# Three of ScalarE's steps cut into parts, and all steps of a hybrid state-space layer placed anew

## The reference

```python
x = x + mamba(layernorm(x))      # D_INNER 256, D_STATE 16, D_CONV 4
x = x + ffn(layernorm(x))
x = x + min_gru(layernorm(x))    # 128 -> 512 -> 128
x = x + ffn(layernorm(x))        # the same weights again
# mamba
xi, z = split(layernorm(x) * gamma + beta @ W_in)
u = silu(conv4(xi) + b_conv)                     # causal, over time
dt = softplus(dt_r @ W_dt + b_dt)                # dt_r, B, C from u @ W_x
h[t] = exp(dt[t] * A) * h[t-1] + dt[t] * u[t] * B[t]
y = (sum over the 16 states of h * C + u * Dskip) * silu(z)
return x + y @ W_out                             # x: mamba's own input
# min_gru
x_in, x_skip = silu(x @ W1 + b1), silu(x @ W2 + b2)
z = sigmoid(x_in @ Wz + bz); h~ = x_in @ Wh + bh
h[t] = (1 - z[t]) * h[t-1] + z[t] * h~[t]        # over time
return (x_skip + h) @ Wo + bo
# ffn: ternary linear 128 -> 512, gelu, ternary linear 512 -> 128,
# each on its input over its root mean square
```

## Time and profile before

| | before |
|---|---|
| median of 3 runs | 849.8 us (848.09 to 851.16) |
| profiled execution | 848.36 us, span 846.6 us |
| instructions | 12621 |
| PE, DVE busy | 705.0 us (83%), 684.5 us (81%) |
| ACT, POOL busy | 641.2 us (76%), 580.7 us (69%) |
| granted PE clock, mean | 0.915 of 2.4 GHz |
| start of the first and of the last scan | 33.92 us, 733.27 us |

### The profile page before, as it was taken

One profiled execution on the slowest core, in us unless ns is written; L12 is line 12 of the kernel. 1 busy time (PEld: TensorE's weight loads), 2 busy tenths in 40 slices (PEclk: granted clock), 3 DMA queues, 4 the chain that ended last, 5 costly groups with the idle time before them and its releaser, 6 DMA issues. The chain is left out here.

```text
span 846.6 us, 12621 instructions
## 1 busy us (share of the span) xinstructions
PE 705.0 (83%) x4116; PEld 596.5 (70%) x4116; DVE 684.5 (81%) x1069; ACT 641.2 (76%) x968; POOL 580.7 (69%) x369
## 2 busy tenths in 40 slices
PE   5666575799789988799789979899799978997995
PEld 4455465578677876588667868688677957786794
DVE  5699989789977998899988998899779988653232
ACT  5787877796899879986899778988898568526403
POOL 4399868777778687877887877968786667513410
PEclk9666677999899999999999999999899979998998
DMA  5521221121111211021112111121111111000000
GB/s 131 184 61 56 75 53 58 51 61 50 32 51 60 63 50 51 27 85 42 50 40 63 63 39 52 41 72 39 50 43 60 50 48 40 2 1 2 13 1 13
DMA packets 35186, 42.81 MB, mean 51 GB/s; under 512 B 7457, under 2 KB 17074, under 8 KB 35122
## 3 DMA queue, kind: packets, MB, share of 16 engines
q1 hardware_dynamic: 35122, 42.00, 16.4%
HBM read 39.63 MB, written 2.36 MB: 50 GB/s over the span
## 5 line engine op out<-in xcount | busy, mean ns | idle before, releaser
L514 POOL TENSOR_TENSOR inflow<-dtu,b_all 128x1024 f32<-128x1024 f32 x127 | 307.7, 2429 | 66.1 <-DVE state L1119 46.6
L1119 DVE TENSOR_TENSOR_SCAN state<-dA,inflow 128x512 f32<-128x512 f32 x256 | 298.3, 1207 | 24.9 <-ACT dA L866 24.5
L866 ACT ACTIVATE dA<-dt,decay_c 128x512 f32<-128x512 f32 x256 | 170.1, 686 | 62.1 <-DVE state L1119 61.2
L1136 DVE TENSOR_TENSOR state<-state,c_ps 128x1024 f32<-128x1024 f32 x128 | 155.6, 1215 | 18.0 <-PE c_ps L1432 13.5
L1441 PE MATMUL y_ps<-ident,state 128*128 128x128 f32 x1024 | 152.2, 298 | 0.0
L1441 PEld LDWEIGHTS y_ps<-ident,state 128*128 128x128 f32 x1024 | 136.1, 155 | 13.9 <-issue 3.8
L1432 PE MATMUL c_ps<-xd,pick 128*128 128x512 f32 x128 | 64.6, 505 | 75.9 <-DVE state L1136 75.8
L1323 PE MATMUL work<-in_hi,wzh_hi 128*128 128x512 f32 x256 | 105.0, 410 | 0.2 <-POOL in_lo L676 0.2
L1324 PE MATMUL work<-in_hi,wzh_lo 128*128 128x512 f32 x256 | 101.3, 396 | 0.0
L1325 PE MATMUL work<-in_lo,wzh_hi 128*128 128x512 f32 x256 | 101.2, 395 | 0.0
L1432 PEld LDWEIGHTS c_ps<-xd,pick 128*128 128x128 f32 x128 | 26.0, 203 | 95.9 <-DVE state L1136 91.3
(11 more groups left out here) (172 smaller groups left out, 1508.3 us busy)
## 6 DMA issues: line engine op xcount, KB each, us to landing
b_all<-b_scratch SPq DMA_DIRECT2D x128, 256.0 KB, 3.2
x_tok<-in_x SPq DMA_DIRECT2D x8, 256.0 KB, 3.7
out_x<-x_tok SPq DMA_DIRECT2D x8, 256.0 KB, 3.6
wide<-in_Wz SPq DMA_DIRECT2D x1, 1024.0 KB, 7.4
...
```

The lines of the kernel that those rows point to most:

```text
L514: eng.tensor_tensor(inflow[:, n % 2, :, tok(b)], dtu[:, :, tok(b)], b_all[:, n % RING, tok(b)].unsqueeze(1).broadcast_to([P, HALVES, TO[b] ...
L866: act.activation(dA[:, h, tok(b)], dt[:, b % 2, h, tok(b)], ACT.Exp, scale=decay_c[:, h, n:n + 1]).then_inc(s_dA[h], 1)
L1119: dve.tensor_tensor_scan(state[:, g % 3, h, tok(b)], dA[:, h, tok(b)], inflow[:, n % 2, h, tok(b)], first, ALU.mult, ALU.add).then_inc(s_s ...
L1136: dve.tensor_tensor(state[:, g % 3, :, tok(b)], state[:, g % 3, :, tok(b)], c_ps[:, tok(b)].unsqueeze(1).broadcast_to([P, HALVES, TO[b] - ...
```

## The change

The two halves of `mix_h_tok` and of `norm_apply` (two tiles each), the two parts of `mix_taps` (u with the first tap, then two taps) and the three parts of `mix_softplus` become operations of their own with places of their own: `h_tok+`, `apply1+`, `taps0+`, `softplus+e`, `softplus+l` and so on. Row 0's softplus stays as it was. What each instruction computes stays, and so do the counts on each engine, but for ACT's table loads: 99 in place of 97. Then all tables have new numbers, `BANK` among them.

```diff
-            def mix_h_tok(b, r, s):
-                act.wait_ge(s_mnb, b + 1)
-                n_tok_free(r, s)
-                for j in tiles(b):
+            def half_tiles(b, part):
+                half = len(tiles(b)) // 2
+                return tiles(b)[part * half:(part + 1) * half]
+
+            def mix_h_tok(b, part, r, s):
+                if part == 0:
+                    act.wait_ge(s_mnb, b + 1)
+                    n_tok_free(r, s)
+                for j in half_tiles(b, part):
...
+            def mix_softplus_exp(b):
+                it = dt[:, b % 2, :, tok(b)]
                 act.wait_ge(s_sparg, HALVES * b + HALVES)
                 act.activation(it, it, ACT.Exp, scale=-1.0).then_inc(s_spexp, 1)
+
+            def mix_softplus_ln(b):
+                it = dt[:, b % 2, :, tok(b)]
                 act.wait_ge(s_spexp, b + 1)
                 act.activation(it, it, ACT.Ln, bias=1.0).then_inc(s_spln, 1)
...
-    "ud": -1, "w12": 1.25, "wzh0": 2.5,
...
+    "ud": -1, "w12": -28.75, "wzh0": 2.75,
...
-    "a.up0": 1, "a.up1": 2, "a.up2": 1, "a.up3": 2, "out": 0, "a.down": 0, "zin0": 2, "zin1": 0, "norm3": 2,
-    "a.sumsq": 1, "d.up0": 1, "d.up1": 2, "d.up2": 2, "d.up3": 1, "norm2": 1, "d.down": 0, "in0": 1, "in1": 2,
...
+    "a.up0": 1, "a.up1": 2, "a.up2": 2, "a.up3": 0, "out": 0, "a.down": 0, "zin0": 2, "zin1": 0, "norm3": 1,
+    "a.sumsq": 2, "d.up0": 2, "d.up1": 1, "d.up2": 2, "d.up3": 1, "norm2": 1, "d.down": 0, "in0": 1, "in1": 2,
```

More of the change, by code:

```diff
@@ L128 @@
-    ("ACT", "d.square3", 1): 42, ("ACT", "h_tok", 1): -21.25, ("ACT", "hi1", 1): 19, ("ACT", "h", 1): -16,
-    ("ACT", "in7", 1): 27.75, ("ACT", "ln_set", 1): -5.75, ("ACT", "silu_u", 1): -8, ("ACT", "silu_z", 1): -2.5,
-    ("ACT", "softplus", 1): -4, ("ACT", "taps0", 1): -12.75, ("ACT", "taps1", 1): -11.5,
-    ("ACT", "z_copy0", 1): -6.75, ("DVE", "apply", 1): -19.75, ("DVE", "d.out", 1): 43.25,
-    ("DVE", "gate", 1): 16.5, ("DVE", "new2", 1): 35.5, ("DVE", "norm", 1): -27.5, ("DVE", "xd_lo", 1): -5,
[9 rows of a table removed]
@@ new lines @@
+    ("DVE", "hid2", 0): 36.25, ("DVE", "hid3", 0): 36.25, ("DVE", "new2", 0): 34.75, ("DVE", "norm", 0): -28.75,
+    ("DVE", "read", 0): 0.25, ("DVE", "scan", 0): -0.5, ("DVE", "stats1", 0): 17.25, ("DVE", "x1", 0): 17,
+    ("DVE", "x2", 0): 25, ("DVE", "x3", 0): 37.5, ("DVE", "xd_lo", 0): -6.25, ("PE", "a.down+", 0): 24.75,
[8 rows of a table added]
+    ("POOL", "base", 0): -17, ("POOL", "conv1", 0): -12.25, ("POOL", "conv2", 0): -13.25,
+    ("POOL", "conv3", 0): -11.5, ("POOL", "d.sum2", 0): 41.75, ("POOL", "h_lo", 0): -7.75,
@@ new lines @@
+    ("DVE", "new1", 7): 34, ("DVE", "new2", 7): 35.25, ("DVE", "new3", 7): 37.25, ("DVE", "norm", 7): -24.75,
+    ("DVE", "read", 7): 0.5, ("DVE", "stats1", 7): 16.75, ("DVE", "stats2", 7): 29, ("DVE", "stats3", 7): 40.5,
[15 rows of a table added]
+    ("POOL", "a.sum2", 7): 24.75, ("POOL", "a.sum3", 7): 24.75, ("POOL", "base", 7): -4.25,
+    ("POOL", "conv3", 7): -12, ("POOL", "d.rms", 7): 48, ("POOL", "d.sum1", 7): 47, ("POOL", "d.sum2", 7): 47,
+    ("POOL", "d.sum3", 7): 47.5, ("POOL", "h_lo", 7): -15.5, ("POOL", "in_lo0", 7): 30,
[3 rows of a table added]
@@ L232 @@
+    ("POOL", "root", 7): -21.5, ("POOL", "x2b", 7): 27.5,
 }
@@ L983, in _ @@
                     mix_softplus(b)
+                for b in due(r, s, ACT_ON["softplus+e"]):
+                    if b > 0:
+                        mix_softplus_exp(b)
+                for b in due(r, s, ACT_ON["softplus+l"]):
+                    if b > 0:
+                        mix_softplus_ln(b)
                 for b in due(r, s, ACT_ON["ud"]):
```

146 lines of the change are left out of this document (76 added, 70 removed), and 234 rows, old and new, of tables (ACT_AT, BANK, DVE_AT, MOVED).

## The result

| | before | changed |
|---|---|---|
| median | 849.8 us (846.6 to 851.2, 20 runs) | 852.0 us (850.0 to 859.0, 20 runs) |
| ratio | | 1.0036 (95%: 1.0023 to 1.0049) |
| profiled execution | 848.36 us | 854.62 us, span 852.8 us |
| start of the first and the last scan | 33.92, 733.27 | 34.12, 740.89 |

A forecast was written before the change was run, and what follows sets the result against it. No engine was at its limit; DVE was fullest (79.34 of 88 us per steady unit), losing time where it waits or is held. Terms summed to -2.8: 848.36 to 845.6, plus 1.4 for the median, 847.0 us; range 840.5 to 855.5.

The forecast's parts named there:

- Start, +0.3: Up to the first scan: `thr` and `thr_neg` now delay it on DVE, 0.3 us slower; bounds 0 and +1.04.
- Unit 0, -1.4: Unit 0: DVE's waits for a decay (0.66 us) and for PE at `bo_tok` (0.74) go; bounds 0 and -1.4.
- `new2` -1.2: Units 4 to 6, step 2: one scan later, its wait for PE's GRU product goes, 0.4 us each; bounds 0 and -1.2.
- `new1` 0: Units 4 to 6, step 0: a new DVE wait of 1.4 us, offset by the wait at `x1` going.
- `lo3` and `a.ms`, +1.2: Units 2 to 6, ahead of the read: DVE's hole swallowed later, only `n_hi`'s lateness on ACT stays; bounds 0 and 5 x 1.2.
- Third rival, the hole stays open: DVE's hole ahead of `lo3` is not swallowed: 1.24 us in five units, 6.2 slower, 853.2 us; chance 0.24.
- `x2b`, 0: Step 11: `rden_d` freed of POOL's lock, 1.1 us in five units, swallowed by the wait for `c_ps`; bounds 0 and -5.4.
- the first rival, the freed locks: The gain at `rden_d`, 5.4 us, is not swallowed and comes on top: 841.6 us; chance 0.2.
- Softplus 0: Step 13's softplus and the halves: unchanged except in unit 1; a decay between two halves changes nothing, 0 us.
- unit 7's loads 0: Unit 7: two added table loads of 1.28 us lie where PE is full, costing 0; +2.6 if PE waits.
- `conv2` and `conv3`, -0.6: Unit 4, one step later: the second GRU scan is held by POOL about 0.6 us less; bounds +0.5 and -1.6.
- Tail, -1.1: After the last scan: PE's third up groups wait less for gelus, -0.6 in row 7, -0.5 in the last layer; bounds 0 and -1.5.

The follow-up runs named there:

- the second profiles: Changed kernel and kernel before, each run again with nothing edited: 850.07 us, ratio 1.003, and 848.87 us, ratio 1.0003.
- the experiment: Changed kernel with POOL's `root` half a step later, behind `rms_d`, and `d.ms` ahead of its read again: 850.76 us, ratio 1.0039.
- the mixtures: Changed kernel with the old places for rows 4 to 7, then instead for rows 0 to 3: 856.26 us (1.0084) and 866.22 us (1.0198).

## Why the prediction was wrong, point by point

**Start, +0.3: not refuted, and not shown.** First scan at 34.12, 0.2 later; but the second profiles have 34.22 before and 34.19 after, so executions differ by as much as the term. The rounding hid as said; `xd` waited 1.61 us behind it, where it had waited 1.42.

**Unit 0, -1.4: too much, 0 to -1.1.** Both waits, of 0.66 and 0.74 us, are gone. But in the changed kernel's profile DVE waits in their place 0.27, 0.34 and 0.16 us for `c_ps`, 0.84 for `gated` at 83.10 and 0.42 for a decay at 85.45, and the unit is as long as before; in the second it is 68.03. In nine profiles of experiments whose unit 0 is the same program it took 66.7 to 67.2 in seven and 68.1 and 69.6 in two. I had taken "few other waits" in the trace of before as a sign that nothing would swallow the gain; a wait that is not there yet is not in that trace.

**`new2` -1.2, `new1` 0: the sizes right, the sum wrong.** The wait of 0.43 us is down to about 0.2, `new1` waits 0.39 us (376.23) and not 1.4 (by its own rows the sum should have had 1.5), and the wait of 1.27 us ahead of `x1` is gone. Steps 0 to 3 take 23.64 us before and 21.89 after in unit 4, but 21.98 and 21.93 in unit 5 and 21.93 and 21.92 in unit 6. So 1.7 us are gained once, in unit 4, and nothing in units 5 and 6; that the gain is `new1`'s and none is `new2`'s is read from the waits, and no run parts the two.

**`lo3` and `a.ms`, +1.2: the step that failed.** The hole that I priced there is swallowed, and undoing it changes nothing that can be measured. What failed is the argument behind it, that the decay of step 9 and what follows hang on an independent chain which keeps its place. I followed DVE, ACT and POOL through steps 7 to 9 and stopped at the decay of step 9; PE's order, on which the third gelu and with it the decay of step 10 hang, I put at nothing without a reason. There `a.down+` had come ahead of `d.up2` and `acc` behind `a.sumsq`, and undoing the first of the two gives back about 5 us. With it undone the kernel is 3.0 us below the one before (849.17 less 846.19), where the forecast was 2.8 below. That this agrees is partly chance: unit 1 has no term and is 0.6 to 1.8 us longer, unit 3 is 1.0 us shorter where I had a loss, and unit 2 differs between executions by 2.4 us (below).

**Third rival, the hole stays open, 853.2:** near to the measured total for another reason. It named the right mechanism in general terms (ACT loses its lead and DVE and ACT wait for each other), with the wrong place, in front of `lo3`, and the wrong engine at its root.

**`norm`: no term.** I counted it as filler of the hole in units 4 and 5. It brought two small `m_vv` beside POOL's `wide` and `inflow`, where they are held 0.8 (unit 4) to 3.3 us. I had named the granted clock and given it no price; the low stretch then fell on steps 8 and 9 in place of step 7.

**`x2b`, 0: right in units 4 to 6,** and so was the rule of the wait for `c_ps` behind it, which the experiment shows in units 4 and 5; there the first rival, the freed locks, falls. In unit 2 it does not hold. `in_lo` now starts behind `rms_d`, where `x2b` had stood, and holds `rden_d` in some executions and not in others; the difference stays in the unit (below).

**Softplus 0, unit 7's loads 0:** unit 7 is 0.2 us longer as a whole, but its two loads of 1.28 us are not hidden: step 13, where they lie, takes 4.62 us in place of 3.56, and the scan behind it waits 0.97 us for the decay. Step 11, 1.4 us shorter, makes up for it.

**`conv2` and `conv3`, -0.6: wrong sign, +0.4.** Step 4 of unit 4 takes 7.78 us (7.41 before). The `inflow` that now starts beside the GRU's scans, at 396.74, takes 3.17 us and not the 2.4 that I gave it, and the pair of scans 4.50, where it had been 4.12.

**Tail, -1.1: near, -1.4.** Counted from the last scan, the third up group of row 7 comes at 29.51 us (29.79 before) and the last layer's at 99.11 (100.10 before). The rows of after, in PE's timeline, that answer to the earlier trace rows:

```profile
770.40 0.47 PE L1518 MATMUL work<-n_hi,up_t 128*128 128x512 f32 x1 [2.16 <-ACT wide L936]
```

```profile
840.00 0.47 PE L1518 MATMUL work<-n_hi,up_t 128*128 128x512 f32 x1 [1.67 <-ACT gelu_d L936]
```

The second gave what was said; the first hardly did. The order made it and not the banks, as the mixtures showed.

**Why executions of the changed kernel differ.** The hold by 0.02 us goes with the difference in unit 5. A second hold of this kind is in unit 2, where steps 11 and 12 take 14.3 us in the first profile and 16.7 in the second. The timelines of DVE and POOL, first and second profile of the changed kernel:

```profile
257.96 0.17 DVE L1237 TENSOR_SCALAR rden_d<-rms_d 128x4 f32<-128x4 f32 x1 [1.65 <-POOL rms_d L684]
...
257.96 1.31 POOL L688 TENSOR_TENSOR in_lo<-wide,in_hi 128x512 fp32r<-128x512 f32 x1
```

```profile
257.20 1.30 DVE L1237 TENSOR_SCALAR rden_d<-rms_d 128x4 f32<-128x4 f32 x1 [1.65 <-POOL rms_d L684]
...
257.19 1.28 POOL L688 TENSOR_TENSOR in_lo<-wide,in_hi 128x512 fp32r<-128x512 f32 x1
```

Of nine profiles with this order, `rden_d` is held in six, 1.26 to 1.30 us, and step 11 then takes 8.3 to 8.4 us in place of 7.2. PE waits for the `x_tok` behind it, 1.83 us in the second profile and 0.68 in the first; in five of the six its clock then dips and step 12 takes 8.4 us in place of 7.1. In the kernel before, `x2b` starts 0.06 us ahead of `rden_d` in units 2 to 6 of both profiles, and each time `rden_d` is held.

**Not settled.** Whether such holds explain every dip that moves was not shown, and no run removed them alone. Unit 1's loss was not tried: its wait at `x1` grew from 2.05 to 3.29 and 3.06 us in the two profiles. And which part of the 5 us that the order of `a.down+` gave back is its length (1.3 us in unit 5 at full clock) and which is the dips made longer by it, the medians don't tell.
